# Making the projections' norm factor straight from the variance, and starting the second chunk's projections a slot sooner

## The reference, cut to what matters

```python
h  = patches @ tok_W.T + tok_b                       # 640 x 512
xn = (h - mean(h)) / sqrt(var(h) + eps)              # layer norm
hn = xn * rsqrt(mean(xn * xn) + eps) * rms1_w        # RMS norm, eps = 1e-5
z, x, B, C, dt = split(hn @ in_proj_w.T)             # 21 tiles of 128 outputs
dt = softplus(dt @ dt_proj_w.T + b)                  # scan over 10 steps, 16 states a channel:
s  = exp(dt * A) * s + dt * x * B ; y = sum(C * s) + D_skip * x
r  = xn + (y * silu(z)) @ out_proj_w.T               # the residual is the normed xn
r  = r + mlp(rms_norm(r)) ; h = h + r ; out = h + mlp2(layer_norm(h))
```

## Time and profile before

| | us |
|---|---|
| median of three runs (lowest, highest) | 671.52 (671.13, 671.97) |
| profiled execution: its own time | 673.53 |
| profiled execution: span of the core | 671.7 |
| TensorE busy | 631.7 (94%) |
| VectorE busy | 417.6 (62%) |
| GpSimd busy | 429.2 (64%) |
| ScalarE busy | 345.1 (51%) |

### The profile page before, as it was taken

How to read it: one execution, slowest core, us unless ns; L and a number is a source line. 1 busy time by engine, 2 the same in 40 slices (tenths; PEclk the granted TensorE clock), 3 DMA queues, 4 the chain that set the end, 5 groups by cost and what they waited for, 6 DMA issues and landing times.

```text
span 671.7 us, 8616 instructions
## 1 busy us (share of the span) xinstructions
PE 631.7 (94%) x2846; PEld 504.8 (75%) x2846; DVE 417.6 (62%) x532; ACT 345.1 (51%) x772; POOL 429.2 (64%) x244
## 2 busy tenths in 40 slices
PE   4959998799999899999998999999999999999998
PEld 3737765466666667777765777766999998999998
DVE  4077896889887889878898988850322223332132
ACT  4359789348888564334365433422543442653441
POOL 0176874527877999997879987644464463445461
PEclk9878998899999899999999999999999999999999
DMA  8699998369999959999967999534443353244421
GB/s 340 236 358 348 311 303 301 137 211 365 344 363 351 392 198 346 414 354 320 334 257 259 387 343 335 180 121 132 134 143 126 125 158 126 63 128 137 143 68 44
DMA packets 49165, 163.50 MB, mean 243 GB/s; under 512 B 4321, under 2 KB 18529, under 8 KB 48481
## 3 DMA queue, kind: packets, MB, share of 16 engines
q1 hardware_dynamic: 49120, 162.95, 69.5%
HBM read 145.24 MB, written 17.69 MB: 243 GB/s over the span
## 4 chain that ended last, share of the span: by engine, by line
PE 77%; DVE 12%; ACT 4%; issue 3%; DMA 2%; POOL 1%; SPq 0%; DVEq 0%; ACTq 0%
PE work L1001 55%; PE da L1001 15%; PE work L1011 6%; DVE da L790 6%; DVE hs L800 2%; ACT L525 1%; DMA bb<-b_rows 1%; ACT da L551 1%; DMA c_rows<-c_rows 1%; DMA sm<-small 1%; DVE sq L872 1%; DVE a L855 0%; POOL hs L450 0%; DVE sq L888 0%; DVE a L881 0%
## 5 line engine op out<-in xcount | busy, mean ns | idle before, releaser
L790 DVE TENSOR_TENSOR_SCAN da<-da,hs 128x580 f32<-128x580 f32 (+1 forms) x128 | 191.1, 1493 | 42.8 <-POOL hs L450 25.8
L450 POOL TENSOR_TENSOR hs<-dtx,bb 128x1160 f32<-128x1160 f32 (+1 forms) x64 | 171.2, 2677 | 63.6 <-PE work L1011 54.5
L429 POOL TENSOR_TENSOR ws<-wraw,ws 128x1024 fp32r<-128x1024 f32 x40 | 101.4, 2535 | 92.9 <-ACT ws L560 92.9
L1001 PE MATMUL work<-sq,wraw 128*128 128x290 f32 x512 | 127.0, 407 | 4.2 <-DVE gate L941 2.6
L1001 PEld LDWEIGHTS work<-sq,wraw 128*128 128x128 f32 x512 | 96.1, 189 | 34.8 <-issue 5.2
L1001 PE MATMUL work<-hn,win 128*128 128x290 f32 (+1 forms) x336 | 105.7, 465 | 16.8 <-DVE hn L863 8.1
L551 ACT ACTIVATE da<-dt,a_neg 128x261 f32<-128x261 f32 (+1 forms) x256 | 118.2, 493 | 0.0
L800 DVE TENSOR_TENSOR hs<-da,cb 128x580 f32<-128x580 f32 (+1 forms) x128 | 105.3, 823 | 10.4 <-DMA cb<-c_rows 2.5
L1001 PEld LDWEIGHTS work<-hn,win 128*128 128x128 f32 x336 | 66.8, 203 | 51.2 <-issue 27.1
L548 ACT COPY da<-zeros 128x58 f32<-128x58 f32 (+1 forms) x128 | 27.6, 216 | 125.7 <-DVE hs L800 125.5
L560 ACT CAST ws<-wraw 128x1024 fp32r<-128x1024 f32 x48 | 50.3, 1049 | 70.3 <-PE da L1001 34.4
(11 more groups left out here) (98 smaller groups left out, 649.3 us busy)
## 6 DMA issues: line engine op xcount, KB each, us to landing
wraw<-w_stream SPq DMA_DIRECT2D x104, 512.0 KB, 4.1
bb<-b_rows SPq DMA_DIRECT2D x32, 700.0 KB, 7.9
cb<-c_rows SPq DMA_DIRECT2D x32, 700.0 KB, 5.9
bb<-b_rows SPq DMA_DIRECT2D x32, 580.0 KB, 8.3
cb<-c_rows SPq DMA_DIRECT2D x32, 580.0 KB, 6.3
c_rows<-c_rows SPq DMA_DIRECT2D x8, 875.0 KB, 10.6
c_rows<-c_rows SPq DMA_DIRECT2D x8, 725.0 KB, 6.8
win<-w_in SPq DMA_DIRECT2D x4, 1024.0 KB, 13.0
```

Of the source, the lines that this page charges most:

```text
L429: nc.gpsimd.tensor_tensor(ws[:, k % NW, 1, :], wraw[:, split_loads[k] % NRAW, :], ws[:, k % NW, 0, :].bitcast(F32), ALU.subtract).then_inc ...
L450: nc.gpsimd.tensor_tensor(hs[:, u % NH, 0:NQ * n].rearrange("p (n t) -> p n t", t=n), dtx[:, t % 2, 0:n].unsqueeze(1).to_broadcast([P, NQ, ...
L790: nc.vector.tensor_tensor_scan(da[:, j, 0:w], da[:, j, 0:w], hs[:, u % NH, j * w:(j + 1) * w], 0.0, ALU.mult, ALU.add).then_inc(scan_done, 1)
L1001: last = nc.tensor.matmul(dst, w, x, start=(k == 0), stop=(k == len(pairs) - 1))
```

## The change

The two factors of `ln1` and `rms1` are folded into one, 1 / sqrt(v (1 + eps) + eps squared), which goes from v and the unscaled a straight to hn. This factor is made first; the factor for the residual's a is made behind it, and a is scaled in VectorE's `rms1` step, after hn. ScalarE has four activations instead of five, VectorE eight tile operations instead of nine; the two semaphores between them go. The projections wait for the norm of `ln1`. The bank of the mean is freed after hn, that of v after a is scaled. In the list of slots `in_dt` and `in_b 0` of chunk 1 move into slot 16, and everything of chunk 1 behind them moves one slot ahead, up to `("dtp", 1, 6), ("xs", 1, 6)`, which move from slot 32 to slot 31 and leave slot 32 with no matrix work but state sums.

```diff
-    bg += [[("tokc", 1)], [("mean", 1), ("ln1", 1)], [("rms1", 1)], [("in_dt", 1), ("in_b", 1, 0)],
+    bg += [[("tokc", 1)], [("mean", 1), ("ln1", 1)], [("rms1", 1), ("in_dt", 1), ("in_b", 1, 0)],
            [("in_x", 1, 0), ("in_b", 1, 1)], [("in_x", 1, 1)]]
     bg += two_tiles(1, 0) + two_tiles(1, 2) + two_tiles(1, 4)
     bg[-1].append(("in_z", 1, 6))
+    bg.append([("dtp", 1, 6), ("xs", 1, 6)])
...
-    first = [[("dtp", 1, 6), ("xs", 1, 6)], [("xs", 1, 7)], o[0:2], o[2:4]]
+    first = [[], [("xs", 1, 7)], o[0:2], o[2:4]]
...
                 elif kind == "ln1":
 
-                    v, ln, inv = NORMS.index(s), rstd_ln[:, 0:n], rstd[:, 0:n]
+
+                    ln, both = rstd_ln[:, 0:n], rstd[:, 0:n]
                     log_tables()
-                    if v >= 1:
-                        act.wait_ge(norm_done, KD * v)
                     full(act, s)
+                    link(nc.scalar.activation(both, bank(s), ACT.Ln, scale=1.0 + EPS, bias=eps_square))
+                    act.wait_ge(h_done, KD * (c + 1))
+                    nc.scalar.activation(bank(("mean", c)), both, ACT.Exp, scale=-0.5).then_inc(rstd_done, 1)
                     link(nc.scalar.activation(ln, bank(s), ACT.Ln, bias=eps_ap))
-                    nc.scalar.activation(inv, ln, ACT.Exp, scale=-1.0).then_inc(inverse_done, 1)
-                    act.wait_ge(h_done, KD * (c + 1))
-                    nc.scalar.activation(bank(("mean", c)), ln, ACT.Exp, scale=-0.5).then_inc(rstd_done, 1)
+                    nc.scalar.activation(bank(s), ln, ACT.Exp, scale=-0.5).then_inc(rstd_done, 1)
                 elif kind == "rms1":
-                    var = ("ln1", c)
-                    log_tables()
-                    act.wait_ge(scaled_var, c + 1)
-                    link(nc.scalar.activation(rstd[:, 0:n], bank(var), ACT.Ln, bias=eps_ap))
-                    nc.scalar.activation(bank(var), rstd[:, 0:n], ACT.Exp, scale=-0.5).then_inc(rstd_done, 1)
+                    return
...
                 elif kind == "ln1":
-                    dve.wait_ge(inverse_done, c + 1)
-                    nc.vector.tensor_tensor(bank(s), bank(s), rstd[:, 0:n], ALU.mult).then_inc(scaled_var, 1)
-                    dve.wait_ge(rstd_done, NORMS.index(s) + 1)
-                    for k in range(KD):
-                        nc.vector.tensor_tensor(a(c, k), a(c, k), bank(("mean", c)), ALU.mult).then_inc(norm_done, 1)
-                elif kind == "rms1":
-                    v, var = NORMS.index(s), ("ln1", c)
+
+                    v, both = NORMS.index(s), ("mean", c)
                     dve.wait_ge(rstd_done, v + 1)
                     if c >= 1:
                         full(dve, ("in_z", c - 1, KI - 1))
+                        full(dve, ("in_c", c - 1, KI - 1))
                     for k in range(KD):
-                        dve.wait_ge(norm_done, KD * (v - 1) + k + 1)
                         nc.vector.scalar_tensor_tensor(out=hn[:, k, 0:n], in0=a(c, k), scalar=small_ap(S_W1, k),
-                                                       in1=bank(var), op0=ALU.mult, op1=ALU.mult).then_inc(norm_done, 1)
+                                                       in1=bank(both), op0=ALU.mult, op1=ALU.mult).then_inc(norm_done, 1)
+                    dve.wait_ge(norm_done, KD * (v + 1))
+                    dve.sem_inc(free_of(both), 1)
+                elif kind == "rms1":
+
+                    v, var = NORMS.index(s), ("ln1", c)
+                    dve.wait_ge(rstd_done, v + 1)
+                    for k in range(KD):
+                        nc.vector.tensor_tensor(a(c, k), a(c, k), bank(var), ALU.mult).then_inc(norm_done, 1)
                     dve.wait_ge(norm_done, KD * (v + 1))
                     dve.sem_inc(free_of(var), 1)
-                    dve.sem_inc(free_of(("mean", c)), 1)
...
-                    v = NORMS.index(("rms1", c))
+                    v = NORMS.index(("ln1", c))
```

More of the change, by code:

```diff
@@ L221, in build @@
         acc = sb("acc", [P, 2 * TM])
-        cols = sb("cols", [P, 8])
+        cols = sb("cols", [P, 9])
         zeros = sb("zeros", [P, 2 * TM // STEPS])
         eps_ap, w_sum, b_mean, minus_one, tok_bc = (cols[:, 0:1], cols[:, 1:2], cols[:, 2:3], cols[:, 3:4], cols[:, 4:8])
+        eps_square = cols[:, 8:9]
         with ExitStack() as scanned:
@@ L264, in build @@
         h_done, centered, centered2, sq_done = sem("h_done"), sem("centered"), sem("centered2"), sem("sq_done")
-        inverse_done, scaled_var = sem("inverse_done"), sem("scaled_var")
         rstd_done, norm_done = sem("rstd_done"), sem("norm_done")
@@ L770, in _ @@
             nc.vector.memset(minus_one, -1.0)
+            nc.vector.memset(eps_square, EPS * EPS)
             nc.vector.memset(zeros[:, :], 0.0)
@@ L850, in step @@
                 elif kind == "ln1":
-                    dve.wait_ge(inverse_done, c + 1)
-                    nc.vector.tensor_tensor(bank(s), bank(s), rstd[:, 0:n], ALU.mult).then_inc(scaled_var, 1)
-                    dve.wait_ge(rstd_done, NORMS.index(s) + 1)
+                    v, both = NORMS.index(s), ("mean", c)
+                    dve.wait_ge(rstd_done, v + 1)
+                    if c >= 1:
+                        full(dve, ("in_z", c - 1, KI - 1))
+                        full(dve, ("in_c", c - 1, KI - 1))
                     for k in range(KD):
-                        nc.vector.tensor_tensor(a(c, k), a(c, k), bank(("mean", c)), ALU.mult).then_inc(norm_done, 1)
+                        nc.vector.scalar_tensor_tensor(out=hn[:, k, 0:n], in0=a(c, k), scalar=small_ap(S_W1, k),
+                                                       in1=bank(both), op0=ALU.mult, op1=ALU.mult).then_inc(norm_done, 1)
+                    dve.wait_ge(norm_done, KD * (v + 1))
+                    dve.sem_inc(free_of(both), 1)
                 elif kind == "rms1":
@@ L858, in step @@
                     dve.wait_ge(rstd_done, v + 1)
-                    if c >= 1:
-                        full(dve, ("in_z", c - 1, KI - 1))
                     for k in range(KD):
-                        dve.wait_ge(norm_done, KD * (v - 1) + k + 1)
-                        nc.vector.scalar_tensor_tensor(out=hn[:, k, 0:n], in0=a(c, k), scalar=small_ap(S_W1, k),
-                                                       in1=bank(var), op0=ALU.mult, op1=ALU.mult).then_inc(norm_done, 1)
+                        nc.vector.tensor_tensor(a(c, k), a(c, k), bank(var), ALU.mult).then_inc(norm_done, 1)
                     dve.wait_ge(norm_done, KD * (v + 1))
                     dve.sem_inc(free_of(var), 1)
-                    dve.sem_inc(free_of(("mean", c)), 1)
                 elif kind == "rms2":
```

## The result

| | before | after |
|---|---|---|
| median (lowest to highest), 22 runs each, us | 670.82 (668.15 to 674.23) | 666.73 (665.13 to 672.17) |
| ratio, 95% interval | | 0.9947 (0.9933 to 0.9962) |
| profiled execution: span, own time, us | 671.7, 673.53 | 663.7, 665.52 |

The change makes the kernel 0.53% faster, 3.6 us by the ratio (2.5 to 4.5) and 4.1 us by the two medians. The forecast was 8.4 us, a time of 663.2 in a range of 661.3 to 667.8. The gain is less than half of what was forecast. The time lies in the range partly by luck: the kernel before, timed again beside the changed one, came out 0.7 us under the 671.52 from which the forecast counted, and 671.52 x 0.9947 is 668.0.

What follows compares the result with a forecast made beforehand. TensorE was taken as the bound, with idle and half-rate time at the norms; 3.6 (start) + 5.8 (seam) - 1.0 (end of chunk 0's scans) = 8.4 us, from 671.52 to 663.2 us, range 661.3 to 667.8.

Steps and rivals of the forecast that it cites:

- The start: Chunk 0's first projections: hn and TensorE start 1.84 us sooner and no clock fall saves 1.75, together 3.59 us.
- The seam on TensorE: Passage to chunk 1's first projections: gain 5.80 us, 2.61 of idle and 3.19 of clock.
- Rival (a): Clock falls at one or both gaps ahead of the first projections: 664.9 or 666.6 us; chance 0.26.
- The end of chunk 0's scans: At the eighth gate: later state sums delay the output projection by 0.7 to 2.9 us, taken as a 1.0 us loss.
- (b): From the seam on, scans replace TensorE as the bound and all the seam's gain is lost: 667.9 us; chance 0.08.
- (c): The start's gain ends in the transfers of the first units: 666.7 us; chance 0.05.
- rival (f): One more clock fall goes, before the seam (112 to 116 us) or at 222 us: 661.5 us; chance 0.08.
- my sign for the output projection: Chunk 0's output projection was to start at 221.65 - 8.4 = 213.3 us.
- the first projection of chunk 1: A sign at the seam: TensorE's first projection there was to start at 123.8 minus 3.6 = 120.2 us.
- 4.9 us of clock: Half-rate time saved behind TensorE's two gaps: 1.75 us at the start and 3.19 us at the seam.
- (d): Units 31 to 33: C and B rows wait 9.6 us behind sooner weight loads, 672.7 us or more; chance 0.04.
- (e): hn still comes late because something else holds VectorE or ScalarE: 671 us; chance 0.04.

Runs made afterwards that it cites:

- 2: The moved slots with the old norms, against the kernel before: 677.38 us, ratio 1.0088 (1.0071 to 1.0106).
- 10: The new norms and moved slots for chunk 1 alone, chunk 0's norms as before, against the kernel before: 670.71 us, ratio 1.0001.
- 11: The kernel before with the eighth gate put at the head of unit 33, nothing else: 670.54 us, ratio 1.0001 (0.9985 to 1.0017).
- experiment 8: The changed kernel with its first six weight loads issued two slots later on SyncE: 664.85 us, ratio to the kernel before 0.9902.
- experiment 9: The new norms for chunk 0 alone, old slots, against the kernel before: 667.52 us, ratio 0.9961 (0.9943 to 0.9978).
- Experiments 1: The new norms with the old list of slots, against the kernel before: 665.15 us, ratio 0.9915 (0.9893 to 0.9937).
- 7: The changed kernel with the eighth gate heading unit 33 and state sum 14 ahead of chunk 1's first projection: 664.22 us, ratio to the kernel before 0.9904.
- experiment 3: The kernel before with 12 and 16 filler matmuls in TensorE's two gaps ahead of the first projections: 667.38 us, ratio 0.9947.
- 6: The new norms with the old slots and the eighth gate at the head of unit 33: 665.79 us, ratio to the kernel before 0.9918.

## Why the prediction was wrong, step by step

**The start (3.6 us): right in its mechanism.** hn behind the first Exp, 0.66 to TensorE, the gap of 1.7 us, the scaling of a at no cost, and the clock that stays: all as worked out. In the four traces with the old norms and no filling (before, 2, 10 and 11) the granted clock was 0.50 behind the start's gap, in none of the nine with the new ones (one of them with filled gaps). Alone it measured 2.6 us (1.5 to 3.8), which leaves the size of 3.6 just possible. The whole chain down to the mean of chunk 1 keeps it: that matmul starts at 115.4 on average in those four traces and at 112.1 in the nine.

**The seam on TensorE (5.8 us): right, but not worth it.** Idle 4.53 to 1.85, clock up, first projection 1.85 us behind the variance, state sums between the tiles. From the mean's matmul to the end of TensorE's last piece before the output projection it is 102.2 us before (116.78 to the 218.94 of the earlier trace rows) and 96.8 after. Rival (a), a fall at one of the two gaps, did not come in any trace: none behind the start's 1.69 us in eight traces, none behind the seam's 1.85 us in five. The Trainium skill, "TensorE: Matmul & The Clock Gate", section "Why this matters for your kernels", by which short gaps are safe, holds for both of these gaps. It does not hold for every gap of that length: in the trace of the start alone a gap of 1.76 us ahead of the output projection, behind dense matmuls, was followed by a fall.

```profile
216.40 5.84 PE L1035 MATMUL work<-yg,wraw 128*128 128x290 f32 x16 [1.76 <-issue]
...
218.00:220.00 2.00, 2.00 (x6) 0.50 1.03 419
```

**The end of chunk 0's scans (1.0 us): this step failed.** The seam and this term together were put at 4.8 us; alone they measured 0.0 (within 1.2). In TensorE's frame the term is as large as the gain before it, about 5 us instead of 1.0. I worked it out from state sum 29, with 10 more matmuls ahead of it, and took 0.7 to 2.9 us. The sum that VectorE waits for is that of unit 28, with 18 more ahead (`xs` 5 and two tiles of `in_z`), which releases unit 32; unit 33 stands behind unit 32 on VectorE whatever sum 29 does. Counted from chunk 1's mean, sum 28 ends at some 86 us in both kernels, and unit 32 starts no sooner than before. This sum is not the whole of it: the wait for it is 1.78 us, and even without it VectorE, with its own work, would have been only 2.3 us ahead there. And I let the wait for C rows go, because the weight loads go out sooner: they went out sooner too against rows that are needed at the old time, and two such waits stand there now; experiment 8 shows 2.5 us of it.

**The rival that came nearest is (b)**, the scans take TensorE's place and all of the seam's gain is lost, at 667.9 with a chance of 0.08. The loss came as it says, but not "from the seam on": in the changed kernel the chain stays on TensorE until 207.26, and the scans overtake it only at units 32 and 33. The median of 666.7 by itself would also fit (a) or (c); the traces and experiment 9 rule these out. Against rival (b) I had put VectorE's 14 us of room in 88. That room is an average over the stretch. Each unit's scans also depend on the loop from a state sum over GpSimd to the scans four units on, and I had myself put each sum behind more work. Experiments 1 and 7 show the chain go over to the scans as soon as TensorE gets 2 us further.

**The clock, taken from one execution.** Since the clock has two levels, twice what a run's mean granted clock lacks of 1, times its span, gives its time at the lower one: 22.4 us a run over 55 runs of the kernel before, 16.5 us over 22 of the changed one, 5.9 less, which at half rate is at most 3.0 us of work. In the two profiled executions it was 26.9 (clock 0.98) and 13.3 us (0.99), 13.6 less, up to 6.8 of the 8.0 us between them.

The trace before has a fall from 112 to 116 us that the changed kernel's has not; but it comes and goes whatever the kernel, in six of the fourteen traces, behind the same two gaps of 1.70 and 0.87 us, so it is no gain of the change (rival (f)). It is also why my sign for the output projection, 213.3, looked fulfilled at 213.76: the first projection of chunk 1 stood at 117.35 instead of 120.2, by this missing fall and the sooner small input, and what the seam then lost made up for that. That is luck.

I took 4.9 us of clock as there in every run. Holding the clock in both gaps of the kernel before gave 3.5 us (experiment 3), so this term was perhaps 1.4 us too large; the interval reaches 4.8, so this is hardly shown. The larger error is the step above.

**Rivals (c), (d) and (e)** are out: the start came through, the weight loads cost 2.5 us and not 9.6, and hn was on time. What the runs leave open is what the wait for sum 28 costs by itself: the trace puts 1.78 us on it, but a version with sum 28 moved alone was not tried.

## What to carry to other kernels

When a wait goes from the engine that looks like the bound, follow the step that releases the next phase (here the eighth gate) back through every engine that feeds it, unit by unit: a gain on TensorE is worth only what that step gets of it. Work put ahead on one engine pushes back everything that shares its queue; here the norms alone (0.9915) beat norms and moved slots together (0.9947; the two intervals just touch). With the gate moved as well the moved slots reach 0.9893, and 0.9885 with the loads, which the intervals do not part from 0.9915. And a fall of the clock seen in one trace can be a draw: compare the mean clock over many runs before it goes into a sum.

## What the runs showed of the hardware

Gaps of TensorE of 1.69 us at the start (eight traces) and 1.85 us at the seam (five), between stretches of dense matmuls, were followed by no fall of the granted clock; the gaps of 3.5 us and more at the same two places were followed by one each time, eight times in five traces. In between, the length of the gap did not settle it. A gap of 1.76 us in the trace of 9 was followed by a fall (0.50 at 218 to 220 us). The same gap of 2.77 us at the seam was followed by one in the trace of 6 (0.50 at 134 to 136 us) and by none in that of 1 (1.00 at 132 to 136), and a gap of 2.78 us ahead of 59.71 in that of 11 by none (1.00 at 58 to 66). Matmuls that compute nothing, put into the two gaps of 3.55 and 4.53 us, made the unchanged kernel 3.5 us faster (2.3 to 4.8).
